# A depthwise convolution moved to TensorE as diagonal matrices, in a fused Mamba and feed-forward kernel

## The reference, cut to what matters

```
x = x + layernorm(mamba(layernorm(x)))
x = x + layernorm(ffn(layernorm(x)))

mamba(v):
  hidden, gate = split(v @ W_in + b_in)          # 512 -> 2 x 1024
  c = silu(sum_k w[k] * hidden[t - 3 + k] + b)   # 4 taps, depthwise, causal
  dt, B, C = split(c @ W_x)                      # 128, 16, 16
  delta = softplus(dt @ W_dt + b_dt)
  h[t] = exp(delta * A) * h[t-1] + delta * c * B # 1024 channels x 16 states
  y = sum_n h * C + c * d_param
  return (y * silu(gate)) @ W_out + b_out

ffn(v): silu(H v @ W_gate) * (H v @ W_up), H, @ W_down   # 512 -> 2048 -> 512, H a Hadamard transform
```

## Time and profile before

| | us |
|---|---|
| median of 3 runs | 2938.16 (2936.92 to 2941.3) |
| profiled execution, its own time | 2942.68 |
| its span, first to last instruction | 2940.8 |
| TensorE busy | 2611.5 |
| VectorE busy | 2265.1 |
| GpSimd busy | 2086.3 |
| ScalarE busy | 1839.7 |

### The profile page before, as it was taken

The page is one execution under the profiler, slowest core; times in us unless marked ns, Lnnn a source line. Parts: engine busy times, 40 slices in busy tenths (PEclk is TensorE's granted clock), DMA queues, the critical chain, the costliest instruction groups (busy, mean ns, idle before and its releaser), DMA issues.

```text
span 2940.8 us, 46415 instructions
## 1 busy us (share of the span) xinstructions
PE 2611.5 (89%) x16064; PEld 2203.8 (75%) x16064; DVE 2265.1 (77%) x2552; ACT 1839.7 (63%) x3968; POOL 2086.3 (71%) x1716
## 2 busy tenths in 40 slices
PE   2556677999999999999999999999999999989997
PEld 0135556887888888887878888888878887877786
DVE  7807888888888888888888888887888888888321
ACT  1337676667776666767676776676676767655221
POOL 6228786978778787868787877878686878776121
PEclk8866998999999999999999999999999999999998
DMA  5741212565665656556656566566566565556586
GB/s 212 264 154 50 62 49 98 200 211 193 222 204 202 215 206 209 205 201 210 210 188 219 205 206 215 201 212 208 199 213 209 187 214 204 203 176 218 201 314 230
DMA packets 163741, 573.60 MB, mean 195 GB/s; under 512 B 17458, under 2 KB 19891, under 8 KB 129716
## 3 DMA queue, kind: packets, MB, share of 16 engines
q1 hardware_dynamic: 163508, 570.64, 56.1%
HBM read 536.49 MB, written 34.08 MB: 194 GB/s over the span
## 4 chain that ended last, share of the span: by engine, by line
PE 60%; DVE 16%; ACT 7%; issue 4%; POOL 3%; DMA 2%; POOLq 0%; DVEq 0%; ACTq 0%; SPq 0%
PE pF L656 17%; PE hT L584 10%; PE pM L597 10%; PE pD L669 8%; DVE h L1012 8%; PE pM L638 7%; DVE acc L1023 5%; POOL dbx L1142 2%; PE decay L656 2%; DMA wug<-scratch_ug 1%; PE pM L612 1%; PE pM L606 1%; ACT L842 1%; PE hT L576 1%; PE pM L640 1%
## 5 line engine op out<-in xcount | busy, mean ns | idle before, releaser
L1012 DVE TENSOR_TENSOR_SCAN h<-decay,dbx 128x512 f32<-128x512 f32 x1024 | 1203.6, 1208 | 321.3 <-ACT decay L842 256.9
L1142 POOL TENSOR_TENSOR dbx<-u,bb 128x2048 f32<-128x2048 f32 (+1 forms) x272 | 1176.9, 4328 | 93.0 <-DVE h L1012 90.9
L842 ACT ACTIVATE decay<-delta,a_neg 128x255 f32<-128x255 f32 x2048 | 870.3, 467 | 201.9 <-DVE h L1012 195.2
L656 PE MATMUL pF<-fxT_hi,wug 128*128 128x256 f32 x3840 | 751.3, 289 | 5.7 <-DMA wug<-scratch_ug 3.6
L1023 DVE SCALAR_TENSOR_TENSOR acc<-hT,bcT,acc 128x1024 f32<-128x1024 f32 x480 | 607.7, 1266 | 93.6 <-PE hT L584 91.8
L584 PE MATMUL hT<-ident,h 128*128 128x128 f32 x4096 | 553.2, 279 | 127.0 <-DVE acc L1023 107.9
L584 PEld LDWEIGHTS hT<-ident,h 128*128 128x128 f32 x4096 | 480.8, 144 | 241.3 <-issue 156.8
L656 PEld LDWEIGHTS pF<-fxT_hi,wug 128*128 128x128 f32 x3840 | 617.1, 192 | 8.0 <-DMA wug<-scratch_ug 5.3
L656 PE MATMUL pF<-fxT_lo,wug 128*128 128x256 f32 x1920 | 544.3, 284 | 0.0
L597 PE MATMUL pM<-xnT,w_in 128*128 128x256 f32 x2048 | 493.6, 385 | 8.1 <-ACT hid L780 3.4
L597 PEld LDWEIGHTS pM<-xnT,w_in 128*128 128x128 f32 x2048 | 376.9, 194 | 53.4 <-ACT hid L780 5.4
(11 more groups left out here) (115 smaller groups left out, 2632.7 us busy)
## 6 DMA issues: line engine op xcount, KB each, us to landing
wug<-scratch_ug SPq DMA_DIRECT2D x256, 1024.0 KB, 4.8
wd<-scratch_wd SPq DMA_DIRECT2D x256, 512.0 KB, 4.0
w_in<-in_W_in SPq DMA_DIRECT2D x256, 256.0 KB, 2.9
bb<-scratch_bc SPq DMA_DIRECT2D x128, 256.0 KB, 4.9
scratch_ug<-split_hi SPq DMA_DIRECT2D x8, 1024.0 KB, 6.2
scratch_ug<-split_lo SPq DMA_DIRECT2D x8, 1024.0 KB, 6.8
xb<-in_hidden_states SPq DMA_DIRECT2D x16, 512.0 KB, 5.0
xr<-in_hidden_states SPq DMA_DIRECT2D x16, 512.0 KB, 5.4
```

What stands on the lines that cost most here:

```text
L656: mm = pe.matmul(gate_up_bank(no)[:, which, :], wug[no % 2][:, 2 * which + a, kt, :], fxT[b][:, kt, :], start=(kt == 0 and i == 0), stop=( ...
L842: e = act.activation(da[q % 2][:, i, 1:], delta[c % 2][:, dt, 1:], ACT.Exp, scale=a_neg[:, dt, n:n + 1])
L1012: dve.tensor_tensor_scan(row(h[n % 2][:, tiles, :]), row(da[q % 2][:, :, :]), row(dbx[n % 2][:, tiles, :]), 0.0, ALU.mult, ALU.add).then_i ...
L1142: pool.tensor_tensor(dbx[n % 2][:, tiles, :], u[:, tiles, :], rows, ALU.mult).then_inc(done if restarts(c) else prod_done, 1)
```

## The change

The conv's four taps become four matrices [128 x 128] for each tile of 128 channels, with the tap's weights on the diagonal; the host lays them out. They come over the same ring as the pieces of `W_in`, which now has 6 buffers, and `in_proj` multiplies them with the hidden tile at four shifts, accumulating in `pM`. ScalarE evacuates the sum with the bias (`conv_out`). `conv_taps`, `add_taps`, the tiles `tap` and `taps` go away. The transposes of x go in two halves through `pM` at slots 30 and 31 of the chunk before, in place of `hT` at slot 0. The tables move the other uses of `pM`: conv at 8 to 11, out projection to 12 to 17, x, B and C to 18 and 19, dt to 20 to 23, gate to 24 to 29. SiLU is issued at slot 12, softplus at slot 24, the rounding of the feed-forward product (`high`) one slot later, the SiLU of the gate one slot earlier, and the norm statistics some slots later.

```diff
-        RING = 4
+        RING = 6
...
-        M_AFTER_FRONT = [("hid", i) for i in range(4)]
+        M_CONV = [("hid", i) for i in range(4)] + [("conv", i) for i in range(4)]
+        M_TURN = [("x", i) for i in range(2)]
...
+        PE_PROJ = {0: ("hid", 0, range(0, 2)), 1: ("hid", 0, range(2, 8)), 2: ("hid", 1, range(0, 2)), 3: ("hid", 1, range(2, 8)),
+                   4: ("hid", 2, range(0, 2)), 5: ("hid", 2, range(2, 8)), 6: ("hid", 3, range(0, 2)), 7: ("hid", 3, range(2, 8)),
+                   8: ("conv", 0, range(8)), 9: ("conv", 1, range(8)), 10: ("conv", 2, range(8)), 11: ("conv", 3, range(8))}
+        PE_OUT = {12: range(0, 2), 13: range(2, 6), 14: range(6, 9), 15: range(9, 13), 16: range(13, 15), 17: range(15, 18)}
+        PE_DT = {20: 0, 21: 1, 22: 2, 23: 3}
+        PE_GATE = {24: (0, range(0, 2)), 25: (0, range(2, 8)), 26: (1, range(0, 2)), 27: (1, range(2, 8)),
+                   28: (2, range(8)), 29: (3, range(8))}
+        PE_TURN = {30: 0, 31: 1}
...
+        ACT_CONV = {9: 0, 10: 1, 11: 2, 12: 3}
+        ACT_OUT = {15: 0, 18: 1}
+        ACT_DT = {21: 0, 22: 1, 23: 2, 24: 3}
+        ACT_GATE = {26: 0, 28: 1, 29: 2, 30: 3}
+        SP_PIECES = {2: ("hid", 3), 4: ("conv", 0), 6: ("conv", 1), 8: ("conv", 2), 9: ("conv", 3),
+                     10: ("gate", 0), 11: ("gate", 1), 12: ("gate", 2), 26: ("gate", 3),
+                     28: ("next", 0), 29: ("next", 1), 30: ("next", 2)}
...
                 load_x(1)
-                load_pieces("hid", 0, 2)
                 load_pieces("hid", 0, 3)
-                load_pieces("hid", 1, 0)
+                for pair in range(4):
+                    load_pieces("conv", 0, pair)
+                for pair in range(3):
+                    load_pieces("hid", 1, pair)
                 sp.dma_start(w_out[:, :, :], W["W_out"].rearrange("(k p) n -> p k n", p=P)).then_inc(loaded_late, 16)
...
-                    if k == 25:
+                    if k == 21:
                         store_bc(front)
...
-            def turn_x(j):
-                pe.wait_ge(xn_done, TB * (j + 1))
-                begin_t(("x", j, 0))
-                for kt in range(KT):
+            def turn_x(j, i):
+                if i == 0:
+                    pe.wait_ge(xn_done, TB * (j + 1))
+                begin_m(("x", j, i))
+                for a in range(2):
+                    kt = 2 * i + a
...
+                        if kind == "conv":
+                            pe.wait_ge(m_evac, M_NO["hid", j, pair] + 1)
...
-                    mm = pe.matmul(pM[:, a, :], w[:, kt, :], xnT[j % 2][:, kt, :], start=(kt == 0), stop=(kt == KT - 1))
+                    src = hid[:, 2 * pair + a, kt:kt + T] if kind == "conv" else xnT[j % 2][:, kt, :]
+                    mm = pe.matmul(pM[:, a, :], w[:, kt, :], src, start=(kt == 0), stop=(kt == KT - 1))
...
-            def conv_taps(j, dt):
...
+            def conv_out(j, pair):
+
+                if pair == 0 and j >= 2:
                     act.wait_ge(y_gated, j - 1)
-                act.wait_ge(m_evac, M_NO["hid", j, dt // 2] + 1)
-                if DT * j + dt >= 2:
-                    act.wait_ge(tap_added, HALO * (DT * j + dt - 1))
-                act.activation(conv[j % 2][:, dt, :], hid[:, dt, HALO:], ACT.Identity, scale=taps[:, dt, HALO:HALO + 1],
-                               bias=b_conv[:, dt:dt + 1])
-                for k in range(HALO):
-                    e = act.activation(tap[dt % 2][:, k, :], hid[:, dt, k:k + T], ACT.Copy, scale=taps[:, dt, k:k + 1])
-                e.then_inc(tap_done, 1)
+                full(("conv", j, pair))
+                for a in range(2):
+                    dt = 2 * pair + a
+                    e = act.activation(conv[j % 2][:, dt, :], pM[:, a, :], ACT.Identity, bias=b_conv[:, dt:dt + 1])
+                e.then_inc(m_evac, 1)
...
-                if k >= 4 and k % 2 == 0 and ff is not None:
-                    high(ff, (k - 4) // 2)
...
+                if k >= 5 and k % 2 and ff is not None:
+                    high(ff, (k - 5) // 2)
...
+                if front is not None:
+                    if k == 12:
+                        conv_silu(front)
+                    if k == 24:
+                        softplus(front)
+                    if k == 31:
+                        first_decay(front)
+                if k == 31 and chunk(c + 2) is not None:
+                    xT(c + 2, 0)
...
-            def add_taps(j, dt):
-
-                pool.wait_ge(tap_done, DT * j + dt + 1)
-                for k in range(HALO):
-                    no = HALO * (DT * j + dt) + k
-                    if k:
-                        pool.wait_ge(tap_added, no)
-                    pool.tensor_tensor(conv[j % 2][:, dt, :], conv[j % 2][:, dt, :], tap[dt % 2][:, k, :], ALU.add).then_inc(tap_added, 1)
```

More of the change, by code:

```diff
@@ L486, in slot @@
             def slot(c, k, cur, front, back, ff, fold):
-                if k == 0 and front is not None:
-                    load_pieces("hid", front, 1)
                 if k == 1 and chunk(c + 2) is not None:
                     load_x(c + 2)
[L491 to L498, removed]
+                if k in SP_PIECES:
+                    kind, pair = SP_PIECES[k]
+                    j = {"hid": front, "conv": front, "gate": cur, "next": chunk(c + 2)}[kind]
+                    if j is not None:
+                        load_pieces("hid" if kind == "next" else kind, j, pair)
                 if cur is not None and k % 4 == 2 and 2 <= k <= 22:
@@ L674, in slot @@
                 n, tb = divmod(k, 2)
[L675 to L686, removed]
@@ L721, in slot @@
-                if front is not None:
-                    x_proj(front, PE_XPROJ.get(k, ()))
+                if k == 0 and fold is not None:
+                    down(fold, HT - 3)
+                if k == 1 and ff is not None:
+                    turn_f(ff)
+                if k == 1 and front is not None:
+                    in_proj(PE_PROJ[1][0], front, *PE_PROJ[1][1:])
+                if k in (2, 3) and back is not None:
+                    turn_y(back, k - 2)
+                if k == 2 and ff is not None:
+                    up_gate(ff, 0)
@@ L731, in slot @@
                         dt_proj(front, PE_DT[k])
+                if back is not None:
+                    out_proj(back, PE_OUT.get(k, ()))
+                if cur is not None and k in PE_GATE:
+                    in_proj("gate", cur, *PE_GATE[k])
+                if chunk(c + 2) is not None and k in PE_TURN:
+                    turn_x(c + 2, PE_TURN[k])
             def front0():
                 pe.wait_ge(loaded, 16 * NLOAD)
-                turn_x(0)
-                for pair in range(4):
-                    in_proj("hid", 0, pair, range(2 * KT))
+                for i in range(2):
+                    turn_x(0, i)
+                for kind in ("hid", "conv"):
+                    for pair in range(4):
+                        in_proj(kind, 0, pair, range(2 * KT))
                 pe.wait_ge(loaded_late, 16 * (NLATE + 1))
-                x_proj(0, range(DT))
+                x_proj(0)
                 bc_proj(0)
@@ L1307 @@
             a = a.T
+        elif short == "conv_w":
+            taps = a.reshape(KC, DT, P).transpose(1, 2, 0)
+            a = np.zeros((DT, P, KC, P), a.dtype)
+            a[:, np.arange(P), :, np.arange(P)] = taps.transpose(1, 0, 2)
         elif short == "W_in":
```

216 lines of the change are left out of this document (82 added, 134 removed).

## The result

The changed kernel takes 3153.93 us (median of 4 runs), the one before 2939.73 us (median of 4). One run of the changed kernel (3413.97 us) had a lower granted clock, 0.83, and is left out of the ratio, which is 1.0715, 95% interval 1.0696 to 1.0735. The profiled execution took 3155.3 us with a span of 3153.5 us, 212.7 us more than before; the sum had +182.

A forecast was written before the change was run, and what follows sets the result against it. TensorE was taken to bound the steady chunks. To the 2940.8 us span it added 169 (chunks 2 to 14), -6 (chunks 0 and 1) and 19 (start): 3122.8, adjusted to 3120 us, range 3058 to 3168.

The forecast's parts named there:

- The bound: Steady chunks of the kernel before: TensorE busy 155.7 of 161 us, 5.3 us idle, nothing else within 20 us of the period.
- 64 records at 0.2155 us: Conv on TensorE, each chunk: 32 fp32 matmuls, two records each, at the input projection's price, 13.8 us.
- Rival C: Conv matmuls with diagonal weights cost about 0.12 us each, 3.8 us a chunk, inside the idle; 2951 to 3000 us; 2%.
- D: Rival: kernel gets faster if a conv record costs under 0.067 us; 2882 us if records cost nothing; 2%.
- +13.0 a chunk: Chunks 2 to 14: conv's 13.8 us less about 0.8 of idle; +169 us over 13 chunks, bounds 113 and 212.
- 0.8 us less: Steady chunks: net fall in TensorE's idle, from waits that go and a new one at the x transpose's second half.
- Rival A: TensorE fills its idle in steady chunks, so +8.7 us a chunk; 3064 us in all; 10%.
- B: Rival: new waits beside the conv, from shared-bank handovers and SyncE ring loads; +16.3 us a chunk, 3163 to 3180 us; 8%.
- SyncE costs nothing: SyncE's queue: 8 more 256 KB loads a chunk, covered by several us of room over the 4.8 us landing.
- Chunks 0 and 1, -6: First two loop chunks: lighter GpSimd and ScalarE shorten six states, together -6 us; bounds -20 and +10.
- The start, +19: Before the loop: conv pairs, table load and SiLU +14, then x projection waits for w_out; +19 us, bounds +14 and +22.
- The end, 0.: Last chunks, which have no conv: no change, 0 +-4 us.

## Why the prediction was right, and where it was off

The direction, the size and the cause hold: 3153.9 us in a range of 3058 to 3168, 34 us over the 3120 forecast. Some 10 us of the miss are in chunks 2 to 14, some 20 in chunks 0 and 1.

- **The bound.** TensorE at 155.7 of 161 us and a chain of its records: right. The straight line of 164.3, 174.6 and 188.2 us over three amounts of conv shows it.
- **64 records at 0.2155 us.** Right: 0.212 to 0.216. Rival C, the cheap diagonal, and D, faster, are out. So is the 3.5 us by the issue gap alone. The four passes of "FP8 and Floating Point Precision" in the Trainium skill, TensorE Precision Notes, fit the slope: the prediction's estimate from them was 0.436 us a matmul, the slope is 0.42 to 0.43.
- **+13.0 a chunk.** +13.8 measured; this term was mis-sized by 0.8 us, 10 us in all. The conv's records were right (13.8). The "0.8 us less" of idle has no sum behind it: the terms written there, 0.89 going and 1.2 coming, give 0.3 more. What came is 0.5 less, partly by luck. The rounding's move was put at nothing beside a busy TensorE; alone it brings 1.35 us. The 1.2 us at the second half of the x transpose did not come: TensorE's down matmuls stand before it, and no such wait is in the trace. In its place stands a wait not foreseen, the down projection at slot 0 behind GpSimd's queue, worth 1.7 us when avoided. The other 0.45 us are the slower other records, which were put at nothing. Rival A is out, and so is B as written: no handover of the bank shows in the steady chunks.
- **SyncE costs nothing.** Nearly: waits for down weights of 0.3 us a chunk came in, and taking them away gave nothing that can be told.
- **Chunks 0 and 1, -6.** The step that failed, in sign: +13.5, outside its own bounds of -20 to +10. The six states it speaks of are, by what they hold, slots 8 to 19. They were forecast to go from 51 to 47.5 us in chunk 0 and from 52 to 50 in chunk 1; they went from 48.4 to 55.6 and from 50.2 to 56.4. The two conv states were right, 17.7 us for "near 9" each, and so was slots 14 to 17 at VectorE's pace in chunk 0. Two terms failed. The state that now holds SiLU was counted among those that fall to VectorE's pace (9 + 9 + 8.9 and three of 6.9 make the 47.5), and took 11.1 us. The state of x, B and C was put at 8.9 us, and took 13.1 and 11.9. The relief itself was also worth less than forecast, since the states before were 2 to 3 us shorter than assumed.
- **The start, +19.** +21.1 (20.5 to 24.9 with the four other traces of that start), with the bank's pitch of 4.65 us and w_out as the last release; 6.7 of it come back when w_out goes first.
- **The end, 0.** -0.8.

## What to carry to other kernels

Ask first which engine's work fills the period: moving 17 us of GpSimd and 11 us of ScalarE work a chunk to the engine that sets the time cost its full 13.8 us (12.1 with the down projection in a better place), and the reverse move, a 2 us bias off TensorE, gave its full 2.3. Stretches with another limit need their own sum, state by state: in chunks 0 and 1 a stall of ScalarE and one long projection took more than the lighter GpSimd gave. A diagonal fp32 matrix pays the dense price. When an instruction becomes the first of its slot, look at what stands in the queues of those who feed it; an ordering that no one paid for before can cost more than the edit's own savings.

## What the runs showed of the hardware

The fp32 matmul of 128x256 with a diagonal weight and a moving operand that starts 0 to 3 elements into its row keeps the pitch of the dense, aligned one: 16 records in 3.46 us in steady chunks, 0.216 us each, and 379 against 387 ns in modelled length. In the steady chunks TensorE stayed at its full 2.4 GHz with the added work, but for 31 us of 2096 in eight short stretches (mean granted clock 0.99; before, 14 us of 1930). In loop chunk 0, from 310 to 330 us, TensorE was busy 14.1 of 20 us and the mean granted clock was 0.52, near the 1.2 GHz level; the x projection's 16 records, from 325.5 us on, took 5.32 us in place of 3.45.
